# A reordering at both ends of the first gate and up stage: scale of h, slots of Wd's sums, half a row of plain products, W's fourth chunk

## The chip, the cores and the metric

The kernel runs on one core of a Trainium2 chip (trn2). The metric is the device time of one execution in microseconds, from runs on the chip; the profile is of one such execution. TensorE does the matrix products, VectorE, ScalarE and GpSimd the rest, and SyncE issues the transfers in the order of its program. Each engine executes its own instructions strictly in order and waits on semaphores.

## What is computed

For x of 8 × 256 tokens with 1024 features:

```
base   = x W^T                                   (1024 -> 1024)
logits = x Wr^T + 5 * one_hot(id)                (8 experts), top 2, softmax -> gates
y      = base + 2 * sum over experts of gate * (x A^T) B^T
h      = silu(y Wg^T) * (y Wu^T)                 (1024 -> 3584)
out    = x + h Wd^T                              (3584 -> 1024)
```

All of it has to come out at close to single precision. The large matrices Wg, Wu and Wd hold float16 values; y and h do not, so each is split into a high and a low float16 part.

## The kernel before

The 2048 tokens are worked in four blocks b = 0 to 3 of T = 512 columns. The order on TensorE is: routing and base of block 0, routing of block 1, then for each b the gate and up products (first_gateup for b = 0, gateup for the others), the base of block b + 1, and down(b).

**Gate and up.** There are 28 units n of two chunks of 128 rows (row 0 and row 1): an even unit has rows of Wg, an odd one of Wu. Each row takes eight matmuls 128x512 with the high part y_hi. The product with the low part y_lo is done in two ways. Units 0 to 15 do it plainly, eight more matmuls 128x512 a row. Units from PLAIN = 16 on do the two rows together by a scheme of seven block products (four matmuls 128x256 each), for which VectorE first makes sums of weight blocks (weight_sums, tile mixed) and of y_lo's blocks (y_sums, y_blocks): products_12, products_34 and products_576. Between them ScalarE takes two results out of PSUM (copy_12: into m1 and m32), VectorE combines (cross_34: into m32 and m45; cross_45: into m45), and GpSimd adds m1 and m32. product_high(n, 0) and product_high(n, 1) do the high products; the one for row 1 waits for cross_45 (s_45). complete(n, 0) and (n, 1) add the cross sums, and product() makes h in single precision (hf).

Unit 15 is plain but stands at the change of scheme: its low products come first, then plain_high(15, 0), products_12(16), plain_high(15, 1), products_34(16). products_12(16) waits for VectorE's first half of y_blocks (s_sum), products_34(16) for ScalarE's two copies (s_copy).

**Sums of Wd.** During units 3 to 14 VectorE also makes 20 sums of blocks of Wd (down_weight_sum, numbered 0 to 19) into the WD_SUMS = 4 slots of wd_sum, sum i into slot i % 4, and SyncE stores each to DRAM. Slots 2 and 3 stand at 174 and 177.5 KB, where m1, m32 and m45 lie (174 to 181 KB); slots 0 and 1 stand at 114 and 200 KB. So ScalarE waits, ahead of copy_12(16), until the last stores of slots 2 and 3 (sums 18 and 19) have landed. Sums 15 and 16 are made in step s = 12, sums 17 and 18 in step 13, sum 19 in step 14. Ahead of the load of x_raw SyncE waits for all of them (down_sums_stored).

**Scale of h.** h of block 0 gets a power of two from the largest weight. ScalarE sums squares of each unit's weights, VectorE takes the largest (own_weight, step 25), GpSimd reduces over partitions (L2203, s_wall), and VectorE makes scales from it (largest_weight, six short operations that first wait for s_wall). rescale(m) applies the scale to hf[m], high (late_high on ScalarE) makes h's high part and low (late_split on VectorE) the low one: 0 to 3 in the last step, 4 to 27 spread over base(1), by LATE. h_sums and last_h_sums then make the sums that down(0) needs.

**base(1).** W is loaded in chunks of 128 rows into four slots. Chunks 0 to 2 come early (EARLY_W = 3), chunk 3 is loaded once unit 27's products are all done (load_w(1, 3) waits for s_g and s_u), and chunk o >= 4 once the chunk that held its slot (o - 4) has been used. ScalarE scales a chunk (w_high, L1845 and L1846), GpSimd makes its low part (w_low, L2160), and TensorE does 24 matmuls with it (L875 to L877). Behind chunk 2 comes turn(1) (transposes, L774), then ScalarE's turned_high (L1876) and VectorE's turned_low (hgT_lo, L1303), which the matmuls of lora (L905 to L907) need.

Names in the profile: L958, L959 and L968 are plain products (L968 low ones of unit 15), L981 plain_high, L988 a block of the scheme, L1035 product_high, L1058 and L1065 the products of down.

Of the kernel before, what the change touches and what calls it, by code (L numbers as in the profile page):

```python
# [5 lines left out]
P = 128  # L6
# [9 lines left out]
F16 = mybir.dt.float16  # L16
# [23 lines left out]
WD_SUMS = 4  # L40
# [9 lines left out]
def adaln_ffn(nc, xT, ids, W, WrT, AT, BT, Wg, Wu, Wd, outT):  # L50
    NB, _, KC, _ = xT.shape
    OC = W.shape[0]
    MC = Wg.shape[0]
# [34 lines left out]
    MH = MC // 2  # L88
# [61 lines left out]
    with ExitStack() as ctx:  # L150
# [3 lines left out]
        def sb(name, kb, shape, dt):  # L154

            return nc.alloc_sbuf_tensor_at(name, shape, dt, offset=base_at + int(kb * KB))
# [27 lines left out]
        x_raw = sb("x_raw", 102, [P, KC, T], F32)  # L184
        x_lo = sb("x_lo", 102, [P, KC, T], F32R)
        wd_half = sb("wd_half", 86, [P, 2, 2, MC, P], F16)
        wd_sum = [sb(f"wd_sum{i}", kb, [P, MH, P], F16) for i, kb in enumerate((114, 200, 174, 177.5))]
        pieces = [sb(f"piece{i}", 135 + 3.5 * i if i < 2 else 86 + 3.5 * (i - 2), [P, MH, P], F16)
                  for i in range(PIECE_SLOTS)]
        xr = sb("xr", 103.5, [P, XR, T], F32)  # L190
# [517 lines left out]
        def _(pe):  # L708
# [231 lines left out]
            def first_gateup():  # L940
                for n in range(PLAIN - 1):
                    pe.wait_ge(d_gu[GU_SLOT[n]], 32 * GU_LOADS[n])
                    if n == 0:
                        for k in range(KC):
                            pe.wait_ge(s_ylo, k + 1)
                            for row in range(2):
                                bank, w, done = chunk(n, row, True)
                                MM(bank, w[:, k, :], y_hi[:, k, :], start=(k == 0), stop=False, skip_group_check=True)
                                mm = MM(bank, w[:, k, :], y_lo[:, k, :], start=False, stop=(k == KC - 1),
                                        skip_group_check=True)  # L950
                                if k == KC - 1:
                                    mm.then_inc(done, 1)
                        continue
                    unit_free(n)
                    for row in range(2):
                        bank, w, done = chunk(n, row, True)
                        for k in range(KC):
                            MM(bank, w[:, k, :], y_hi[:, k, :], start=(k == 0), stop=False)  # L958
                            mm = MM(bank, w[:, k, :], y_lo[:, k, :], start=False, stop=(k == KC - 1))  # L959
                        mm.then_inc(done, 1)  # L960

                n = PLAIN - 1
                pe.wait_ge(d_gu[GU_SLOT[n]], 32 * GU_LOADS[n])
                unit_free(n)
                for row in range(2):
                    bank, w, done = chunk(n, row, True)
                    for k in range(KC):
                        mm = MM(bank, w[:, k, :], y_lo[:, k, :], start=(k == 0), stop=False, skip_group_check=True)  # L968
                mm.then_inc(s_plain, 1)
                plain_high(n, 0)  # L970
                products_12(PLAIN)
                plain_high(n, 1)
                products_34(PLAIN)
                products_12(PLAIN + 1)
                products_576(PLAIN)
                by_blocks(PLAIN, MC)

            def plain_high(n, row):
                bank, w, done = chunk(n, row, True)
                for k in range(KC):  # L980
                    mm = MM(bank, w[:, k, :], y_hi[:, k, :], start=False, stop=(k == KC - 1), skip_group_check=True)  # L981
                mm.then_inc(done, 1)

            def block(bank, second, w, y, first):

# [158 lines left out]
        def _(dve):  # L1144
# [251 lines left out]
            def rescale(m):  # L1396
                V.tensor_scalar(hf[:, m], hf[:, m], wmax[:, 2:3], None, ALU.mult).then_inc(s_rs, 1)
# [204 lines left out]
            def first_gateup():  # L1602
                for s in range(MC):
                    blocks_next = PLAIN <= s + 1 < MC
                    if s == MC - 1:
                        rescale(0)
                        late_split(0, FIRST_LATE)
                    if s == PLAIN - 1:
                        dve.wait_ge(s_plain, 1)
                        y_blocks()  # L1610
                    if s >= PLAIN - 1:
                        for u in SUM_AT.get(s, ()):
                            weight_sums(u)
                    if blocks_next:
                        cross_34(s + 1)
                    if s == MC - 3:
                        own_weight()
                    if s >= PLAIN:
                        complete(s, 0)
                        complete(s, 1)  # L1620
                    elif s % 2:
                        for m in (s - 1, s):
                            dve.wait_ge(s_u, m + 1)
                            product(0, m, hf[:, m])
                    if s == MC - 2:

                        largest_weight()
                    if blocks_next:
                        cross_45(s + 1)
                    if s < PLAIN - 1:  # L1630
                        for u in SUM_AT.get(s, ()):
                            weight_sums(u)
                    if s == Y_SUMS_AT:
                        y_sums(0)
                    for q, c in DOWN_SUMS.get(s, ()):
                        down_weight_sum(q, c)
                    if s == SCALES_AT:
                        fine_scales()
# [171 lines left out]
        def _(act):  # L1810
# [79 lines left out]
            def late_high(first, end):  # L1890
                for m in range(first, end):
                    act.wait_ge(s_rs, m + 1)
                    if m >= WORK:
                        act.wait_ge(s_hlo, m - WORK + 1)
                    high(m, hf[:, m])

            def base(b):
                if b == 1:
                    late_high(FIRST_LATE, 6)
                else:  # L1900
                    route(b)
                w_high(b, 3)
                if b == 1:
                    late_high(6, 8)
                w_high(b, 4)
                if b == 1:
                    late_high(8, 9)
                turned_high(b)
                if b == 1:
                    late_high(9, 11)  # L1910
                w_high(b, 5)
                if b == 1:
                    late_high(11, LATE[0])
                for o in range(OC):
                    copy_chunk(b, o)
                    if o in (3, 4):
                        w_high(b, o + 3)
                    if b == 1:
                        late_high(LATE[o], LATE[o + 1])
                    if b == 0 and 2 <= o < 6:  # L1920
                        x1_high(2 * o - 4)
                        x1_high(2 * o - 3)
# [93 lines left out]
            def first_gateup():  # L2016
                for s in range(MC):
                    if 0 < s < PLAIN:
                        for u in SUM_AT.get(s, ()):
                            sum_squares(u)  # L2020
                    if s >= PLAIN:
                        if s % 2 == 0:
                            act.wait_ge(s_fix, 2 * nth(s) - 1)
                            silu(0, s)
                        if s + 2 < MC:
                            copy_12(s + 2)
                        if s % 2 == 0:
                            act.wait_ge(s_fix, 2 * nth(s))
                            silu(0, s + 1)
                        for u in SUM_AT.get(s, ()):  # L2030
                            sum_squares(u)
                    elif s % 2 == 0:
                        for m in (s, s + 1):
                            act.wait_ge(s_g, m + 1)
                            silu(0, m)
                    if s == 0:
                        sum_squares(0)
                    if s == PLAIN - 1:

                        for i in range(2, WD_SUMS):  # L2040
                            act.wait_ge(d_dsum[i], 16 * 5 * PAIRS // WD_SUMS)
                        copy_12(PLAIN)
                        copy_12(PLAIN + 1)
                    q, j = divmod(s - 1, 3)
                    if 0 <= q < PAIRS:
                        for i in ((0,), (1, 2), (3,))[j]:
                            halve_down(q, i)
                    next_parts(s)

                act.wait_ge(s_m6, nth(MC - 2))  # L2050
                act.wait_ge(d_mixed[2], 16 * mixed_stores(2))
                late_high(0, FIRST_LATE)
# [199 lines left out]
```

## Time and profile before

| | |
|---|---|
| time, median of 3 runs | 1331.1 us (1330.82, 1331.10, 1332.72) |
| time of the profiled execution | 1330.87 us |
| its span, first to last instruction | 1329.0 us |
| TensorE matmul busy | 1320.0 us (99% of the span), 8540 instructions |
| VectorE / ScalarE / GpSimd busy | 794.6 / 408.6 / 132.4 us |
| mean granted clock of TensorE | 0.998 |
| the chain that ended last | TensorE 98%, VectorE 1%, issue 1% |

The profiled execution took 1.87 us more than its span; that lies around the first and the last instruction. Times inside the profile are microseconds from the start of the span. The granted clock is the share of full speed (2.4 GHz) that the throttle let TensorE have: 1.00 is 2.4 GHz, 0.50 is 1.2 GHz.

### The profile page before, as it was taken

The page shows a single profiled execution, that of the slowest core. Times are in us where ns is not written, and L with a number is a line of the kernel's source. Part 1 is how long each engine was busy: PE and PEld are TensorE (multiplying, and loading weights), DVE is VectorE, ACT ScalarE, POOL GpSimd, SP SyncE. Part 2 cuts the span into 40 slices and gives each one's busy share as a digit, 9 for nine tenths or more (in the row PEclk, how much of TensorE's full clock was granted, in tenths as well). Part 3 has the DMA queues.
Part 4 walks back from the last instruction along what each step waited for, and adds up shares of the span by engine and source line. Part 5 has one row for each costly group of instructions (what it writes and reads, how often), then busy time and mean ns, then how long its engine had stood idle before and what let it go on. Part 6 is the DMA issues. An engine that isn't in the chain of part 4 may idle for free.

```text
span 1329.0 us, 22089 instructions
## 1 busy us (share of the span) xinstructions
PE 1320.0 (99%) x8540; PEld 860.5 (65%) x8540; DVE 794.6 (60%) x1540; ACT 408.6 (31%) x705; POOL 132.4 (10%) x163
## 2 busy tenths in 40 slices
PE   9999999999999999999999999999999999999999
PEld 7854456545666666677667666667666666666666
DVE  7798888678614577764742555556473255545612
ACT  4368845563101344321011223332110122222000
POOL 3200202241000011100000111110000011111000
PEclk9999999999999999999999999999999999999999
DMA  8379985225955778853794568653387465666564
GB/s 309 119 258 358 410 310 180 76 80 198 320 203 157 275 256 322 314 183 111 262 322 157 186 223 275 185 165 114 103 310 268 144 186 184 186 181 205 172 233 137
DMA packets 117528, 287.00 MB, mean 216 GB/s; under 512 B 14128, under 2 KB 16816, under 8 KB 116656
## 3 DMA queue, kind: packets, MB, share of 16 engines
q1 hardware_dynamic: 117136, 285.43, 62.7%
q8 instruction: 68, 1.11, 0.4%
q14 instruction: 36, 0.29, 0.1%
q10 hardware_dynamic: 288, 0.16, 0.0%
HBM read 241.24 MB, written 44.30 MB: 215 GB/s over the span
## 4 chain that ended last, share of the span: by engine, by line
PE 98%; DVE 1%; issue 1%; DMA 0%; POOL 0%; ACT 0%; DVEq 0%; ACTq 0%; POOLq 0%
PE banks L1035 25%; PE banks L988 22%; PE banks L1058 14%; PE banks L1065 13%; PE banks L782 4%; PE banks L959 3%; PE banks L958 3%; PE banks L834 2%; PE banks L878 1%; PE banks L880 1%; PE banks L879 1%; PE banks L875 1%; PE banks L877 1%; PE banks L876 1%; PE banks L1094 1%; PE banks L718 1%
## 5 line engine op out<-in xcount | busy, mean ns | idle before, releaser
L1035 PE MATMUL banks<-y_hi,gu_ring 128*128 128x512 f16 x1504 | 355.7, 381 | 2.8 <-DVE m L1662 2.8
L1035 PEld LDWEIGHTS banks<-y_hi,gu_ring 128*128 128x128 f16 x1504 | 147.3, 98 | 143.2 <-DVE m L1662 3.3
L1058 PE MATMUL banks<-h,piece 128*128 128x512 f16 x840 | 188.5, 380 | 0.0
L1935 ACT ACTIVATE sg<-banks,sc 128x512 f32<-128x512 f32 x112 | 76.4, 686 | 211.6 <-DVE banks L1671 153.6
L2181 POOL TENSOR_TENSOR m<-m,m 128x256 f32<-128x256 f32 x96 | 69.7, 726 | 717.4 <-DVE m L1652 717.3
L1058 PEld LDWEIGHTS banks<-h,piece 128*128 128x128 f16 x840 | 82.1, 98 | 89.8
L1674 DVE TENSOR_TENSOR banks<-banks,m 128x256 f32<-128x256 f32 x96 | 41.5, 432 | 137.2 <-PE banks L1035 137.0
L1065 PE MATMUL banks<-h,piece 128*128 128x256 f16 x896 | 106.2, 273 | 0.0
L1065 PEld LDWEIGHTS banks<-h,piece 128*128 128x128 f16 x896 | 87.6, 98 | 19.8
L988 PE MATMUL banks<-y_lo,gu_ring 128*128 128x256 f16 x752 | 97.5, 273 | 1.5 <-ACT m L2065 1.5
L2064 ACT COPY m<-banks 128x256 f32<-128x256 f32 x96 | 35.3, 368 | 173.0 <-PE banks L988 166.8
L988 PE MATMUL banks<-y_sum,mix_c 128*128 128x256 f16 x672 | 87.1, 273 | 0.0
L1652 DVE TENSOR_TENSOR m<-banks,m 128x256 f32<-128x256 f32 x96 | 40.3, 420 | 68.0 <-PE banks L988 68.0
L988 PEld LDWEIGHTS banks<-y_lo,gu_ring 128*128 128x128 f16 x752 | 73.4, 98 | 11.2 <-issue 2.0
L959 PE MATMUL banks<-y_lo,gu_ring 128*128 128x512 f16 x208 | 79.0, 380 | 0.0
L958 PE MATMUL banks<-y_hi,gu_ring 128*128 128x512 f16 x208 | 79.0, 380 | 0.0
L1065 PE MATMUL banks<-h_sum,piece 128*128 128x256 f16 x672 | 78.6, 273 | 0.0
L1888 ACT ACTIVATE h<-work 128x512 f16<-128x512 f32 x84 | 52.9, 630 | 82.0 <-DVE work L1599 82.0
L1065 PEld LDWEIGHTS banks<-h_sum,piece 128*128 128x128 f16 x672 | 65.7, 98 | 7.7
L988 PEld LDWEIGHTS banks<-y_sum,mix_c 128*128 128x128 f16 x672 | 65.7, 98 | 7.7
L2097 ACT ACTIVATE d<-banks 128x256 f32<-128x256 f32 x16 | 6.1, 379 | 204.1 <-PE banks L1065 191.0
L1599 DVE SCALAR_TENSOR_TENSOR work<-banks,sc,sg 128x512 f32<-128x512 f32 x84 | 63.1, 751 | 3.0
(239 smaller groups left out, 1959.3 us busy)
## 6 DMA issues: line engine op xcount, KB each, us to landing
piece<-down_dram SPq DMA_DIRECT2D x80, 448.0 KB, 5.5
mix_c<-mix_dram SPq DMA_DIRECT2D x84, 384.0 KB, 4.0
piece<-Wd SPq DMA_DIRECT2D x64, 448.0 KB, 5.4
gu_ring<-Wu SPq DMA_DIRECT2D x110, 256.0 KB, 3.3
gu_ring<-Wg SPq DMA_DIRECT2D x108, 256.0 KB, 3.2
mix_a<-mix_dram SPq DMA_DIRECT2D x84, 256.0 KB, 2.7
mix_dram<-mixed SPq DMA_DIRECT2D x28, 640.0 KB, 5.1
wb<-w_dram SPq DMA_DIRECT2D x64, 256.0 KB, 3.7
```

The source lines that it names most:

```text
L782: mm = MM(bank[:, at], w[a][:, k, :], x[:, a, k, :], start=(first and a == 0 and k == 0), stop=False, skip_group_check=True)
L958: MM(bank, w[:, k, :], y_hi[:, k, :], start=(k == 0), stop=False)
L959: mm = MM(bank, w[:, k, :], y_lo[:, k, :], start=False, stop=(k == KC - 1))
L988: mm = MM(bank[:, at], w[:, k, :], y[:, k, :], start=(first and k == 0), stop=False, skip_group_check=True)
L1035: mm = MM(bank, w[:, k, :], y_hi[:, k, :], start=False, stop=(k == KC - 1), skip_group_check=True)
L1058: mm = MM(bank, w[:, k, :], h[:, half * MH + k, 0, :], start=(start and k == 0), stop=False, skip_group_check=True)
L1065: mm = MM(bank[:, at], w[:, k, :], y[:, k, :], start=(start and k == 0), stop=False, skip_group_check=True)
L1599: V.scalar_tensor_tensor(out=tile, in0=banks[:, chunk_bank(b, m, 1), :], scalar=sc[:, b, 2:3], in1=sg[:, n % SG, :], op0=ALU.mult, op1=ALU ...
L1674: V.tensor_tensor(odd_1, odd_1, m45[:, n % 2], ALU.add).then_inc(s_fix, 1)
L1888: S.mul(h[:, m, 0, :], source, 1.0 / LO_SHIFT).then_inc(s_hhi, 1)
L1935: S.activation(sg[:, n % SG, :], banks[:, chunk_bank(b, m, 0), :], ACT.Silu, scale=sc[:, b, 1:2]).then_inc(s_sg, 1)
L2181: G.tensor_tensor(m1[:, n % 3], m1[:, n % 3], m32[:, n % 2], ALU.add).then_inc(s_1236, 1)
```

## The change

Four things are moved; no instruction is added or removed.

1. The four slots of wd_sum trade places: slots 0 and 1 now stand where m1 and m32 lie, slots 2 and 3 at 114 and 200 KB; ScalarE waits ahead of copy_12(16) for the stores of slots 0 and 1.
2. TensorE does the first four of the eight matmuls of plain_high(15, 1) ahead of products_12(16), and the other four behind it.
3. VectorE calls largest_weight at the start of the last step (s = 27), behind cross_45(27), where it stood ahead of cross_45(27).
4. In base(1) ScalarE scales W's chunk 3 ahead of late_high(4) to late_high(7), where it stood between 5 and 6.

```diff
-        wd_sum = [sb(f"wd_sum{i}", kb, [P, MH, P], F16) for i, kb in enumerate((114, 200, 174, 177.5))]
+        wd_sum = [sb(f"wd_sum{i}", kb, [P, MH, P], F16) for i, kb in enumerate((174, 177.5, 114, 200))]
...
-                plain_high(n, 0)
+                plain_high(n, 0, 0, KC)
+                plain_high(n, 1, 0, KC // 2)
                 products_12(PLAIN)
-                plain_high(n, 1)
+                plain_high(n, 1, KC // 2, KC)
                 products_34(PLAIN)
...
-            def plain_high(n, row):
+            def plain_high(n, row, first, end):
                 bank, w, done = chunk(n, row, True)
-                for k in range(KC):
+                for k in range(first, end):
                     mm = MM(bank, w[:, k, :], y_hi[:, k, :], start=False, stop=(k == KC - 1), skip_group_check=True)
-                mm.then_inc(done, 1)
+                if end == KC:
+                    mm.then_inc(done, 1)
...
                     if s == MC - 1:
+
+                        largest_weight()
                         rescale(0)
                         late_split(0, FIRST_LATE)
...
-                    if s == MC - 2:
-
-                        largest_weight()
                     if blocks_next:
                         cross_45(s + 1)
...
             def base(b):
-                if b == 1:
-                    late_high(FIRST_LATE, 6)
-                else:
+                if b == 0:
                     route(b)
                 w_high(b, 3)
                 if b == 1:
-                    late_high(6, 8)
+                    late_high(FIRST_LATE, 8)
                 w_high(b, 4)
...
                     if s == PLAIN - 1:
 
-                        for i in range(2, WD_SUMS):
+                        for i in range(2):
                             act.wait_ge(d_dsum[i], 16 * 5 * PAIRS // WD_SUMS)
                         copy_12(PLAIN)
```

## Rows read from the trace of the kernel before

**Rows 1.** Waits of TensorE, whole execution: total us, times, longest.

```profile
PE banks L1035 <- DVE m L1662: 2.8, 1, 2.8
PE banks L988 <- ACT m L2065: 1.5, 1, 1.5
```

**Rows 2.** Windows: length, busy PE, PEld, DVE, ACT, POOL, then clock, DMA, GB/s.

```profile
184.00:190.00 6.00, 5.00 (x41) 3.89 (x42) 3.98 (x10) 1.32 (x4) 0.72 (x1) 1.00 0.81 292
260.69:263.65 2.96, 0.16 (x1) 0.00 (x1) 1.51 (x8) 0.00 (x0) 0.41 (x1) 0.91 0.00 0
263.65:266.78 3.13, 3.13 (x8) 1.13 (x9) 2.75 (x7) 1.78 (x3) 0.00 (x0) 0.54 0.00 0
266.78:271.94 5.16, 5.16 (x25) 2.35 (x24) 5.05 (x11) 1.94 (x4) 0.00 (x0) 1.00 0.33 102
```

**Rows 3.** Timeline, 178 to 186 us: start, us, engine, line, operation, [idle before, releaser].

```profile
178.48 1.89 PE L981 MATMUL banks<-y_hi,gu_ring 128*128 128x512 f16 x8
...
180.60 0.61 PE L988 MATMUL banks<-y_sum,mixed 128*128 128x256 f16 x4 [0.23 <-DVE y_lo L1373]
...
181.49 1.89 PE L981 MATMUL banks<-y_hi,gu_ring 128*128 128x512 f16 x8
...
183.59 0.42 DVE L1582 TENSOR_TENSOR mixed<-halved 128x512 f16<-128x512 f16 x1
184.09 0.37 ACT L2064 COPY m<-banks 128x256 f32<-128x256 f32 x1 [6.29 <-DMA down_dram<-wd_sum]
...
184.36 0.39 ACT L2065 ACTIVATE m<-banks 128x256 f32<-128x256 f32 x1
...
184.89 1.03 PE L988 MATMUL banks<-y_lo,gu_ring 128*128 128x256 f16 x8 [1.51 <-ACT m L2065]
...
185.96 0.42 DVE L1652 TENSOR_TENSOR m<-banks,m 128x256 f32<-128x256 f32 x1 [1.95 <-PE banks L988]
```

**Rows 4.** Timeline, 172 us: the stores of sums 17 and 18 as issued.

```profile
172.50 1.32 SPq L474 DMA_DIRECT2D down_dram<-wd_sum  x2
```

**Rows 5.** DMA issues from 172.45 and in 255 to 315 us: KB each, us to landing.

```profile
down_dram<-wd_sum SPq DMA_DIRECT2D x2, 448.0 KB, 5.1
...
w_raw<-W SPq DMA_DIRECT2D x5, 512.0 KB, 3.2
```

**Rows 6.** Timeline, 258 to 267 us, around unit 27's last row.

```profile
258.09 1.04 PE L988 MATMUL banks<-y_sum,mixed 128*128 128x256 f16 x8
...
258.96 1.89 PE L1035 MATMUL banks<-y_hi,gu_ring 128*128 128x512 f16 x8
261.49 0.41 POOL L2203 PARTITION_ALL_REDUCE wmax<-wmax  x1 [5.86 <-issue]
...
263.17 0.42 DVE L1662 TENSOR_TENSOR m<-m,banks 128x256 f32<-128x256 f32 x1
...
263.65 3.29 PE L1035 MATMUL banks<-y_hi,gu_ring 128*128 128x512 f16 x8 [2.80 <-DVE m L1662]
```

**Rows 7.** Timeline, 270 to 284 us: VectorE, ScalarE and GpSimd in base(1).

```profile
270.75 0.49 DVE L1397 TENSOR_SCALAR hf<-hf,wmax 128x512 f32<-128x512 f32 x1
...
271.80 1.14 ACT L1845 ACTIVATE w<-w_raw,mx 128x1024 f16<-128x1024 f32 x1
...
274.06 6.78 POOL L2160 TENSOR_TENSOR w<-w_raw,w 128x256 f16<-128x256 f32 x8 [12.17 <-ACT w_raw L1846]
...
275.20 0.89 DVE L1397 TENSOR_SCALAR hf<-hf,wmax 128x512 f32<-128x512 f32 x1
...
283.68 0.75 DVE L1303 SCALAR_TENSOR_TENSOR hgT_lo<-banks,y_sc,hgT_hi 128x512 fp32r<-128x512 f32 x1 [4.62 <-ACT hgT_hi L1876]
```

**Rows 8.** VectorE's timeline, and one piece of the chain of waits.

```profile
313.82 2.03 DVE L1714 TENSOR_TENSOR h_sum<-h 128x3584 f16<-128x3584 f16 x1 [0.69 <-PE banks L877]
...
327.50 1.09 DVE L1727 TENSOR_SCALAR h<-h 128x3584 f16<-128x3584 f16 x1
...
331.11 6.11 PE banks L1065 x56
```

## The prediction

> **What bounds the kernel now.** I read the page first. TensorE is busy 1320.0 us of a span of 1329.0 us (the table above), so the kernel is one long stream of matmuls and only 9.0 us of it are idle. An edit that adds and removes no matmul can win only from those 9.0 us, and from stretches in which the matmuls run slower than elsewhere. The view of waits, kept to TensorE, says where the idle time is [rows 1]: one wait of 2.8 us before the matmuls of L1035 (for VectorE's m45) and one of 1.5 us before those of L988 (for ScalarE's copies). The rest is a start-up, the tail behind the last matmul and a few tenths. Both waits stand in stage b = 0, the edited one. The table of windows then shows what the first wait costs beyond itself [rows 2]: between 260.69 and 263.65 us TensorE does next to nothing, and in the 3.13 us behind it the granted clock is 0.54, so mostly the 1.2 GHz level, under eight matmuls; from 266.78 us it is 1.00 (2.4 GHz) again, 24 matmuls in 5.16 us, 0.216 us each. Behind the 1.5 us wait the clock is 1.00 at once [rows 2]. So the second stall is worth more than its 2.8 us.
>
> **Part one: first blocks (slots of Wd's sums, half a row of plain products).** TensorE begins unit 15's plain high products at 178.48 us, does eight, waits briefly for y_lo and does products_12(16) at 180.60, does the other eight from 181.49, and starts products_34(16) only at 184.89 [rows 3]. That last start waits for ScalarE's pair of copies at 184.09 and 184.36, and ScalarE waited 6.29 us for a store of wd_sum [rows 3]: slots 2 and 3 lie where m1 and m32 are written, and their last user is sum 19, stored last.
> After the edit m1 and m32 lie on slots 0 and 1, last used by sums 16 and 17. The store of 17 is one of the two issued from 172.50 us, which take 5.1 us to land [rows 4, 5]: with 1.32 us for the issuing of both, by 178.9 at the latest. ScalarE then waits for products_12(16) alone. Its new place: 12 matmuls of 0.216 behind 178.48, so 181.07. VectorE's first doubled y_lo released TensorE at 180.60 before, so that wait of 0.23 us goes. Eight matmuls of 0.109 (180.60 to 181.49, with 0.02 of change-over) end at 181.94. From the end of a block to the engine that reads it take 0.20 us (184.89 plus 0.87 is 185.76; VectorE starts at 185.96 [rows 3]): ScalarE starts at 182.14. The two copies take 0.66 us (184.09 to 184.36 + 0.39), and 0.14 us later TensorE started: 182.94. Meanwhile the four plain matmuls that are left run from 181.94 to 182.80 and hide all but 0.14 us of the copies. Gain: 184.89 − 182.94 = **1.95 us**. Without any wait it were 184.89 − 182.80 = 2.09, the upper bound. The lower bound is 0: if sums 16 and 17 landed no sooner than sum 19 did, ScalarE's copies would start at 184.09 as before.
> What is late next? VectorE's cross_34(16) needs TensorE's block, now out at 182.94 + 0.87 + 0.20 = 184.01, and VectorE's sums of the weights end at 183.59 + 0.42 = 184.01 [rows 3]. They meet; a few hundredths at most. SyncE's queue is blocked till the last sum has landed in either version, so the load of unit 20's weights and x_raw stay at 184.1 to 184.5 in absolute time; what uses them is VectorE's work some 9 us and more later, so the shift of 1.95 us costs nothing there.
>
> **Part two: largest_weight behind cross_45(27).** VectorE executes in order. Before, it stood in front of largest_weight until GpSimd's all-reduce, which starts at 261.49, and only after six short operations did it write m45 (263.17), which released TensorE's last row at 263.65 [rows 6]. But m45's own inputs were there early: the seventh product's four matmuls end at 258.09 + 0.44, and 0.20 later, at 258.73, VectorE can do its 0.42 us: 259.15. TensorE reaches the row at 258.96 + 1.73 = 260.69, so 1.5 us later: no wait. The row then runs 260.69 to 262.42 at the full clock, where before the next product began at 266.78. Gain: 2.96 (263.65 − 260.69) for the stall and 3.13 − 1.73 = 1.40 for the clock [rows 2], together **4.36 us**. Bounds: 2.96, if the clock drops all the same; 4.36 above. The stall of 1.5 us that left the clock alone [rows 2] is longer than anything I expect to remain, so I take 4.36.
> By the Trainium skill (TensorE: Matmul & The Clock Gate, What's actually happening) the clock level follows how busy TensorE has recently been, and by its note there the moment of a switch varies from run to run. By that rule some runs of before may have missed the drop, and against those the gain here is 2.96. The rows show one run only, with the drop.
>
> **Does base(1) let the gain through?** The all-reduce at 261.49 follows GpSimd's own last operation by 5.86 us [rows 6], so it should move with the stream; if it stayed where it is in absolute time, VectorE would be 1.95 us later still, which the reserve worked out below would have to bear. As it is, largest_weight ends just before 263.17 as before (first gain left aside), and VectorE's work behind it comes only 0.35 us sooner (m45 has left its place), while TensorE is 4.36 sooner. VectorE is thus 4.0 us later than before relative to TensorE. Who needs it? The products by W of chunks 0 to 2 need neither h nor the split. The turn of hg and VectorE's hgT_lo come next: there VectorE had been idle 4.62 us [rows 7], which pays for the 4.0.
> The fourth chunk of W: its load is issued when TensorE's last row is done, 262.6, and lands 3.2 us later [rows 5], 265.9. Before, late_high of 4 and 5 stood ahead of its scaling on ScalarE, and the scaling began at 271.80, two passes of 1.1 us. Now it comes directly behind late_high(3). VectorE hands over a rescale per 1.0 us from 263.2 on (a rescale and a low part each), so that is about 267.1; the scaling ends at 269.3, and GpSimd's subtraction (3.4, half of the eight in 6.78 [rows 7]) at 272.7. TensorE wants it at 262.42 + 3 × 5.16 = 277.9 at the earliest. Without the move the scaling would follow rescale(5), which VectorE does at 270.4, and GpSimd would be done at about 276.9, still in time: the move is worth nothing by itself.
> But the move puts that GpSimd work beside VectorE's products and splits. A rescale took 0.49 us alone and 0.89 beside GpSimd [rows 7]. Three or four operations with 0.4 each are 1.3 us. Step by step: VectorE's rescale(5) at 270.4, then a pair of operations per 1.0 us, low(8) behind late_high(8) at 276.2, end 276.9 without and about 278.4 with this contention. hgT_lo is due at 283.68 − 4.36 = 279.3. Reserve 0.9 to 2.4 us. Behind it stand 0.69 us of VectorE's wait at h_sum and the time from its last sum, 327.50 + 1.09 = 328.6, to TensorE's L1065 at 331.1, 2.5 us [rows 8]: 3.2 us more before TensorE would feel it. So cost 0.
> By the Trainium skill (SBUF — State Buffer, SBUF: two separate sides) VectorE and GpSimd share a port pair under an exclusive lock, and the loser is blocked for a whole instruction. By it VectorE might lose all 3.4 us, reach hgT_lo 1.0 us late, and use a third of the 3.2 behind it; the sum stays, the reserve shrinks. The trace agrees so far as the rescale's 0.89 for 0.49 goes.
> Behind 316 us all loads and waits hang on TensorE's own progress, so both gains go through to the end.
>
> **Sum.** 1.95 + 4.36 = 6.3 us. The profiled execution took 1330.87 us, of which 1329.0 span: 1324.6 and a span of 1322.7. The median of the runs lies 0.2 higher, so **1324.8 us**.
>
> **Rivals.**
> (a) The first stall stays, since the wait on slots 0 and 1 ends late or VectorE's sums hold cross_34 back. Against it: 3 us of reserve on the stores. 1331.1 − 4.4 = 1326.7. Chance 0.06.
> (b) The clock falls all the same, or part of the runs never had the drop: 1331.1 − 1.95 − 2.96 = 1326.2. For it, the times of before reach from 1330.82 to 1332.72, and only one of its executions shows a clock. Chance 0.05.
> (c) The time goes into base(1): VectorE's chain of splits, which has little idle time there, arrives late and TensorE waits at L1065 for what it had gained. It needs a delay of 0.9 + 3.2 us and more behind what I reckoned, and 4.4 more to take all: 1329.1. Chance 0.06.
> (d) Slower: ScalarE now stands at the chunk's load ahead of all late splits. If it landed late, late_high(4) and so VectorE's chain would stand still with it. From 267.1 on each microsecond goes into the reserve of about 4 (0.9 + 3.2) and then into TensorE's wait. To eat 6.3 and be 2.7 slower it must land 13 us behind 267.1, 17 us after issue instead of 3.2, while the queues are nearly empty there (DMA share 0.33 [rows 2]). At that point 1333.8. Chance 0.02.
> The forecast holds the other 0.81.
>
> **Range.** The forecast's own range is 1324.0 (the last waits gone too, and 0.5 of scatter) to 1325.6. With (a) and (b) it reaches 1327.2; (c) and (d) are left out. A difference under 0.2%, 2.7 us, can't be told from no change here. Faster: forecast, (a), (b), 0.92. Same: (c), 0.06. Slower: (d), 0.02.
>
> **What the profile of the changed kernel would show.** The wait of 2.8 us at L1035 gone from TensorE's waits, that of 1.5 us down to about 0.1 to 0.3; ScalarE's first copy near 182.1, released by TensorE and not by a store; products_34(16) at 182.9; the last row of unit 27 near 258.7 (260.69 − 1.95) with clock 1.00; the first product by W near 260.5; VectorE's idle time before hgT_lo down from 4.62 to between 0.5 and 2.5; TensorE busy 1.4 us less. Wrong would be: a new TensorE wait at L877, L905, L1058 or L1065 between 270 and 330 us, a clock below 1.00 behind 255 us, or a copy still released by wd_sum.

## The result, and the profile after

The changed kernel takes 1325.07 us (median of 6 runs, 1324.31 to 1325.22), the kernel before beside it 1331.0 (6 runs, 1329.53 to 1332.72). The ratio is 0.9954, with a 95% interval of 0.9941 to 0.9967: 5.9 us faster. The forecast was 1324.8.

On the page, TensorE's busy time has gone from 1320.0 to 1317.6 us, with the same 8540 matmuls:

```profile
span 1323.4 us, 22089 instructions
...
PE 1317.6 (100%) x8540; PEld 860.7 (65%) x8540; DVE 793.6 (60%) x1540; ACT 408.9 (31%) x705; POOL 132.1 (10%) x163
```

TensorE's waits over the whole execution, which answer to [rows 1]:

```profile
PE banks L714 <- DVE idle L1772: 1.2, 1, 1.2
PE banks L718 <- DVE x_lo L1179: 0.9, 1, 0.9
```

Both waits of before are gone from the list (ahead of products_34(16) some 0.2 us of idle time are left, 183.30 behind the end of four matmuls from 182.22). What is left is the start-up. In the profiled execution of before the twelve warm-up matmuls (L714) took 5.30 us and covered the second row's wait for x; in this one they took 4.34. That accounts for 1.0 of the 2.4 us of busy time that are gone; the other 1.4 is the slow clock behind the last row. The start-up comes before anything that the change touches. Unit 15's plain high products begin at 178.75 here, where they began at 178.48 [rows 3]: the profiled execution is 0.27 us late before the change begins, so the stages are compared from a start of their own.

**The first blocks.** The timeline, which answers to [rows 3]:

```profile
178.75 2.75 PE L982 MATMUL banks<-y_hi,gu_ring 128*128 128x512 f16 x12
...
181.34 0.60 PE L990 MATMUL banks<-y_sum,mixed 128*128 128x256 f16 x4
...
182.22 1.03 PE L982 MATMUL banks<-y_hi,gu_ring 128*128 128x512 f16 x4
182.49 0.37 ACT L2063 COPY m<-banks 128x256 f32<-128x256 f32 x1 [4.41 <-PE banks L990]
...
182.76 0.39 ACT L2064 ACTIVATE m<-banks 128x256 f32<-128x256 f32 x1
...
183.30 1.03 PE L990 MATMUL banks<-y_lo,gu_ring 128*128 128x256 f16 x8
...
184.37 0.42 DVE L1653 TENSOR_TENSOR m<-banks,m 128x256 f32<-128x256 f32 x1
```

ScalarE's first copy is now released by TensorE (L990), not by a transfer. From the first plain high product to products_34(16) it is 183.30 − 178.75 = 4.55 us, where it was 184.89 − 178.48 = 6.41: 1.86 us gained, 1.95 forecast.

**The last row of unit 27 and base(1).** The timeline, which answers to [rows 6] and [rows 7]:

```profile
256.49 1.04 PE L990 MATMUL banks<-y_sum,mixed 128*128 128x256 f16 x8
...
257.13 0.42 DVE L1663 TENSOR_TENSOR m<-m,banks 128x256 f32<-128x256 f32 x1 [0.44 <-PE banks L990]
257.37 3.62 PE L1037 MATMUL banks<-y_hi,gu_ring 128*128 128x512 f16 x16
259.98 0.41 POOL L2202 PARTITION_ALL_REDUCE wmax<-wmax  x1 [5.95 <-issue]
...
265.60 1.13 ACT L1846 ACTIVATE w<-w_raw,mx 128x1024 f16<-128x1024 f32 x1
...
267.86 3.19 POOL L2159 TENSOR_TENSOR w<-w_raw,w 128x256 f16<-128x256 f32 x4 [7.47 <-ACT w_raw L1847]
...
269.37 1.15 DVE L1404 SCALAR_TENSOR_TENSOR h<-h,hf 128x512 f16<-128x512 f16 x1
...
270.44 0.89 DVE L1399 TENSOR_SCALAR hf<-hf,wmax 128x512 f32<-128x512 f32 x1
...
277.72 0.75 DVE L1305 SCALAR_TENSOR_TENSOR hgT_lo<-banks,y_sc,hgT_hi 128x512 fp32r<-128x512 f32 x1 [1.35 <-ACT hgT_hi L1877]
```

VectorE begins to write m45 at 257.13, before TensorE has begun even the first of the two rows, and is done at 257.55, 1.55 us before the second row begins (1.5 forecast); the sixteen matmuls of both rows stand in one line (x16) with no wait between them. The windows of the two rows and of what follows (columns as in [rows 2]) show the clock at 1.00 throughout:

```profile
257.37:259.10 1.73, 1.73 (x11) 0.79 (x9) 0.18 (x1) 0.04 (x1) 0.00 (x0) 1.00 0.00 0
259.10:260.82 1.72, 1.72 (x9) 0.78 (x8) 0.33 (x3) 0.00 (x0) 0.41 (x1) 1.00 0.00 0
260.82:264.00 3.18, 3.18 (x16) 1.47 (x15) 2.66 (x9) 1.15 (x2) 0.00 (x0) 1.00 0.50 164
```

From the first row's start to the first product by W it is 3.45 us, where it was 266.78 − 258.96 = 7.82: 4.37 us gained, 4.36 forecast. The all-reduce moved with the stream, as assumed: 259.98 − 257.37 = 2.61 us behind the first row, where it was 2.53. And VectorE's idle time before hgT_lo is 1.35 us where it was 4.62, inside the 0.9 to 2.4 forecast; the rows at 269.37 and 270.44 are the operations that GpSimd's earlier work stretches.

**What arrives.** The starts of the four down stages in the chain of waits, first of the kernel before:

```profile
314.42 3.04 PE banks L1094 x14
...
637.83 3.04 PE banks L1094 x14
...
961.23 3.04 PE banks L1094 x14
...
1234.67 3.02 PE banks L1094 x14
```

and of the changed kernel:

```profile
308.49 3.04 PE banks L1096 x14
...
631.89 3.04 PE banks L1096 x14
...
955.30 3.04 PE banks L1096 x14
...
1229.01 3.02 PE banks L1096 x14
```

The lead is 5.93, 5.94 and 5.93 us: it passes base(1) and two whole stages without a loss, and it is the sum of 1.86 and 4.37, less the 0.27 of the late start and 0.03 that I did not place. Between 955 and 1229 another 0.27 us is lost: the stationary loads before a piece's matmuls (L1067) wait 0.4 us there for nothing that the trace names.

### The profile page after: what moved, and what is told of

The parts are those of the page before. It is cut to its first block, busy times and chain, and to the rows that moved or that the text cites. A ratio compares the mean times of both kernels' runs of the same rounds, so it can differ in the third digit from the quotient of the medians.

```text
span 1323.4 us, 22089 instructions
## 1 busy us (share of the span) xinstructions
PE 1317.6 (100%) x8540; PEld 860.7 (65%) x8540; DVE 793.6 (60%) x1540; ACT 408.9 (31%) x705; POOL 132.1 (10%) x163
## 4 chain that ended last, share of the span: by engine, by line
PE 99%; DMA 0%; DVE 0%; SPq 0%; issue 0%; ACT 0%; DVEq 0%
PE banks L1037 25%; PE banks L990 22%; PE banks L1060 14%; PE banks L1067 13%; PE banks L782 4%; PE banks L958 4%; PE banks L959 4%; PE banks L834 2%; PE banks L878 1%; PE banks L880 1%; PE banks L879 1%; PE banks L875 1%; PE banks L876 1%; PE banks L877 1%; PE banks L1096 1%; PE banks L718 1%
## 5 line engine op out<-in xcount | busy, mean ns | idle before, releaser
L1067 PE MATMUL banks<-h,piece 128*128 128x256 f16 x896 | 106.1, 273 | 0.0
L1067 PEld LDWEIGHTS banks<-h,piece 128*128 128x128 f16 x896 | 87.7, 98 | 19.8
L990 PE MATMUL banks<-y_lo,gu_ring 128*128 128x256 f16 x752 | 97.4, 273 | 0.1
L990 PE MATMUL banks<-y_sum,mix_c 128*128 128x256 f16 x672 | 87.1, 273 | 0.0
L990 PEld LDWEIGHTS banks<-y_lo,gu_ring 128*128 128x128 f16 x752 | 73.5, 98 | 9.7 <-issue 0.5
L1067 PE MATMUL banks<-h_sum,piece 128*128 128x256 f16 x672 | 78.6, 273 | 0.1
L1067 PEld LDWEIGHTS banks<-h_sum,piece 128*128 128x128 f16 x672 | 65.7, 98 | 8.0 <-issue 0.4
L990 PEld LDWEIGHTS banks<-y_sum,mix_c 128*128 128x128 f16 x672 | 65.8, 98 | 7.6
```

The source lines that it names most:

```text
L990: mm = MM(bank[:, at], w[:, k, :], y[:, k, :], start=(first and k == 0), stop=False, skip_group_check=True)
L1067: mm = MM(bank[:, at], w[:, k, :], y[:, k, :], start=(start and k == 0), stop=False, skip_group_check=True)
```

## The experiments

The small numbers need the runs' clocks. Each run lists the mean granted clock of its execution, to three digits. Over four sets, the kernel before was executed 69 times beside the experiments: 23 executions have a clock of 1.000 and a median of 1329.56 us (1328.92 to 1330.15); 46 have 0.997 to 0.999 and 1331.30 (1330.59 to 1333.05). There is no overlap. So the kernel before has two times, 1.7 us apart, and its median lies among the commoner ones. The mean clock does not say where in an execution the clock fell. The profiles of before, e5 and e6 show it at the wait ahead of unit 27's last row, and where that wait is gone or filled in whole or half (the changed kernel, e2, e3, e4, e7, e8, e9, e11, e12) no execution is below 1.000, save three of e10, which has long waits of its own. So the fall is put down to that wait in the other executions too; no trace of those shows it.

| kernel | time, us (range, runs) | runs at clock 1.000 | ratio, 95% interval |
|---|---|---|---|
| e1 first blocks only | 1329.24 (1327.85 to 1330.47, 11) | 3 of 11 | 0.9991, 0.9982 to 1.0 |
| e2 largest_weight only | 1326.57 (1326.43 to 1326.97, 6) | 6 of 6 | 0.9968, 0.9956 to 0.998 |
| e3 wait filled, 13 matmuls | 1329.62 (1329.39 to 1330.21, 11) | 11 of 11 | 0.9991, 0.9982 to 1.0 |
| e4 changed kernel again | 1324.65 (1324.44 to 1325.45, 5) | 5 of 5 | 0.9955, 0.9942 to 0.9969 |
| e5 slots only | 1329.88 (1327.48 to 1331.34, 10) | 1 of 10 | 0.9994, 0.9985 to 1.0004 |
| e6 half row only | 1330.97 (1329.34 to 1331.57, 10) | 1 of 10 | 1.0003, 0.9993 to 1.0012 |
| e7 whole row ahead | 1325.35 (1325.13 to 1325.6, 5) | 5 of 5 | 0.9963, 0.9949 to 0.9977 |
| e8 fourth chunk not moved | 1324.75 (1324.33 to 1325.11, 4) | 4 of 4 | 0.9956, 0.9939 to 0.9973 |
| e9 VectorE 3.7 us later | 1324.88 (1324.71 to 1325.13, 4) | 4 of 4 | 0.9958, 0.9942 to 0.9975 |
| e10 VectorE 7.4 us later | 1328.84 (1328.4 to 1329.95, 10) | 7 of 10 | 0.9987, 0.9978 to 0.9997 |
| e11 wait half filled | 1329.51 (1329.02 to 1330.31, 10) | 10 of 10 | 0.9987, 0.9977 to 0.9996 |
| e12 VectorE 5.6 us later | 1326.37 (1326.27 to 1327.07, 5) | 5 of 5 | 0.9962, 0.9948 to 0.9976 |

**The two parts apart, and together (e1, e2, e4).** e1 is the kernel before with items 1 and 2 of the change, e2 the kernel before with item 3:

```diff
                     if s == MC - 1:
+
+                        largest_weight()
                         rescale(0)
...
-                    if s == MC - 2:
-
-                        largest_weight()
```

> The first-blocks part alone (slots of Wd's sums and half a row of plain products), largest_weight and W's fourth chunk left as in the kernel before. My theory: products_34(16) starts 1.9 us sooner behind the first plain high product than before, the 2.8 us wait at the last row and the slow clock behind it stay, time 1331.0 - 1.9 = 1329.1. Rival (the two stalls are one: with the first gone the second grows, since the all-reduce stays where it is in absolute time): last row's wait 4.8 us, time 1331.

> largest_weight behind cross_45(27) alone, all else as before. My theory: wait of 2.8 us gone, clock 1.00 there, first product by W 4.4 us sooner relative to product_high(27, 0), time 1331.0 - 4.4 = 1326.6. Rival (the clock falls there all the same, whatever TensorE waited): 3.0 us sooner, 1328.0. Rival (base(1) gives it back): 1331.

> The changed kernel as it is, beside its parts on the same chip. If the parts add: the gains of the two single parts, 1.9 and 4.4, sum to its 6.3 less the scatter, 1324.8 to 1325.1. Rival (they overlap): less than the sum by over 1 us.

Measured: 1329.24, 1326.57 and 1324.65 beside 1331.1 of before: gains of 1.9, 4.5 and 6.4 us. By these medians the parts add.

The medians mix executions that kept the clock with others, so they have to be compared like with like. In this set the kernel before has 1329.54 at clock 1.000 (8 executions) and 1331.36 below it (14). e2 gains 2.97 us on the first, which is the stall alone, and 4.8 on the second. e1 gains 1.5 us at clock 1.000 (3 executions, 1328.05) and 1.6 below it (8, 1329.72), not 1.9; the changed kernel gains 4.9 and 6.7. So e1's median of 1329.24 is in part the luck of how many of its executions kept the clock.

e1's profiled execution was one that kept it, and shows what the profile of before could not:

```profile
PE banks L1037 <- DVE m L1664: 3.0, 1, 3.0
```

That is its wait; this is the row of matmuls behind it:

```profile
262.23 1.90 PE L1037 MATMUL banks<-y_hi,gu_ring 128*128 128x512 f16 x8 [3.04 <-DVE m L1664]
```

The wait is even 0.24 us longer than in [rows 6], but the eight matmuls take 1.90 us, not 3.29. That fits e1's smaller gain: 1.87 us from its first blocks (178.58 to 183.12 in its trace, 4.54 us) less 0.24 is 1.6. Its all-reduce came 2.76 us behind the first row's start at 257.31, where it came 2.53 behind before:

```profile
260.07 0.41 POOL L2205 PARTITION_ALL_REDUCE wmax<-wmax  x1 [6.09 <-issue]
```

The stall did not grow by the 1.9 us that e1's rival expected. So behind a wait of about 3 us the clock falls in some executions and in others it does not, and the longer of these two waits is the one that left it alone. In e5's profiled execution it fell early and stayed low longer; its windows from the wait on:

```profile
260.90:263.50 2.60, 1.32 (x4) 0.50 (x5) 2.08 (x8) 0.87 (x2) 0.00 (x0) 0.58 0.00 0
263.50:266.00 2.50, 2.50 (x8) 0.85 (x7) 2.50 (x6) 1.50 (x3) 0.00 (x0) 0.50 0.00 0
266.00:268.00 2.00, 2.00 (x6) 0.75 (x5) 1.96 (x4) 0.67 (x2) 0.00 (x0) 0.50 0.51 190
268.00:270.00 2.00, 2.00 (x10) 0.89 (x9) 1.93 (x5) 0.21 (x1) 0.00 (x0) 0.97 0.18 72
```

There the clock is at the 1.2 GHz level until 268, so the first six products by W are slow too. The last row of that profile begins at 262.18 and the first product at full speed at 268.12: fourteen matmuls in 5.9 us, where the full clock needs 3.0, so 2.9 us are lost. In e6's profile two products by W are slow beside the row, and 1.7 us are lost. The price of this one wait thus reaches from 0 to about 3 us beyond the wait, in the four profiles that have it: 0 (e1), 1.4 (before), 1.7 (e6) and 2.9 (e5).

**The wait filled with work (e3, e11).** To part the clock from the wait, useless matmuls into a free bank, ahead of the wait for m45:

```diff
             def product_high(n, row):
                 bank, w, done = chunk(n, row, True)
+                if row and n == MC - 1:
+                    pe.wait_ge(s_wlo, OC)
+                    pe.wait_ge(s_xlo, 2 * KC)
+                    pe.wait_ge(s_hf, MC - 2)
+                    for i in range(13):
+                        MM(banks[:, 7, :], w16[:, 0, 0, i % KC, :], x16[:, 1, i % KC, :], start=True, stop=True)
                 if row:
                     pe.wait_ge(s_45, nth(n))
```

e11 has `range(6)`.

> The kernel before with 13 matmuls 128x512 of no use (into a free PSUM bank) put into the wait ahead of the last row of unit 27; the wait for m45 stays. If the idle time is what lowers the clock: granted clock 1.00 behind it, the eight matmuls of the last row in 1.7 us in place of 3.1, time 1.4 less than before (1329.6), with TensorE busy about 1.4 us more. Rival (the clock falls for another reason there, or the 2.8 us wait alone is the cost): the last row stays at 3.1 us and the time at 1331.0.

> The kernel before with 6 useless matmuls in place of 13 ahead of the last row of unit 27: 1.3 us of the wait are filled, some 1.5 us of idle time stay, as long as the other wait of before (1.5 us at L988), which left the clock alone. My theory: the clock stays at 1.000 in all executions and the time is that of the filled kernel, 1329.6, narrow. Rival (any wait at this place lowers the clock in part of the executions): some executions at 0.998 to 0.999 and 1331, as before.

The timeline of e3 around the wait:

```profile
260.91 2.97 PE L1037 MATMUL banks<-x,w 128*128 128x512 f16 x13
...
263.77 1.90 PE L1041 MATMUL banks<-y_hi,gu_ring 128*128 128x512 f16 x8
```

m45 still comes when it came (the last row starts 4.59 us behind the first one's start at 259.18, where it was 4.69 before), and yet 13 matmuls more make the kernel 1.5 us faster: 1329.62. That is the time of the executions of before that kept their clock, 1329.56. All 11 executions kept it, where 23 of 69 do without the filling. With half the filling (e11) there is a wait again:

```profile
PE banks L988 <- ACT m L2071: 1.5, 1, 1.5
PE banks L1041 <- DVE m L1668: 1.4, 1, 1.4
```

with the row behind it at full speed:

```profile
263.83 1.90 PE L1041 MATMUL banks<-y_hi,gu_ring 128*128 128x512 f16 x8 [1.42 <-DVE m L1668]
```

and all 10 executions keep the clock (1329.51). So at this place the unfilled wait, 2.78 to 3.04 us long where a profile shows it, lowers the clock in 46 of 69 executions, and 1.4 us of idle time in none of ten.

**What in the first blocks does it (e5, e6, e7).** e5 is the kernel before with the slots traded and ScalarE's wait on them, e6 the kernel before with the half row alone, and e7 the changed kernel with

```diff
                 plain_high(n, 0, 0, KC)
-                plain_high(n, 1, 0, KC // 2)
+                plain_high(n, 1, 0, KC)
                 products_12(PLAIN)
-                plain_high(n, 1, KC // 2, KC)
```

> The kernel before with the slots traded (and ScalarE's wait on slots 0 and 1), but no half row. My theory: ScalarE's copies start when products_12(16) is done, near 182.0 us with products_12 at 180.6; products_34(16) starts when the plain row ends, about 4.7 us behind the first plain high product where it was 6.4: gain 1.65 to 1.7 us, so the slots carry nearly all of part one. Rival (the half row is what hides the copies): gain under 1.0.

> The kernel before with half a row of plain products ahead of products_12(16), slots as before. My theory: products_34(16) still starts 0.8 us behind ScalarE's first copy, which the store of sum 19 releases near 184.1: gain 0 (the 0.24 us wait for y_lo goes and comes back in the wait for the copies). Rival: gain 0.2 to 0.4.

> The changed kernel with the whole second plain row ahead of products_12(16), nothing left behind it. My theory: nothing covers the copies, so products_34(16) waits for them: products_12(16) ends at +4.33 us behind the first plain high product, copies end 0.28 + 0.66 + 0.14 later: +5.4 where the changed kernel has 4.55, that is 0.85 us slower than it. Rival (cross_34, not the copies, is the bound): no slower.

Their times scatter with the clock (e5's median is 0.8 us under that of before, e6's 0.3 over it, and both intervals hold 1), so the trace decides. From the first plain high product to products_34(16), e5:

```profile
178.55 1.89 PE L981 MATMUL banks<-y_hi,gu_ring 128*128 128x512 f16 x8
...
183.27 1.04 PE L988 MATMUL banks<-y_lo,gu_ring 128*128 128x256 f16 x8
```

e6:

```profile
178.90 2.75 PE L982 MATMUL banks<-y_hi,gu_ring 128*128 128x512 f16 x12
...
184.47 0.37 ACT L2066 COPY m<-banks 128x256 f32<-128x256 f32 x1 [6.24 <-DMA down_dram<-wd_sum]
...
185.27 1.03 PE L990 MATMUL banks<-y_lo,gu_ring 128*128 128x256 f16 x8 [1.88 <-ACT m L2067]
```

e7:

```profile
178.09 3.62 PE L981 MATMUL banks<-y_hi,gu_ring 128*128 128x512 f16 x16
...
183.50 1.03 PE L989 MATMUL banks<-y_lo,gu_ring 128*128 128x256 f16 x8 [0.92 <-ACT m L2063]
```

These are 4.72, 6.37 and 5.41 us, beside 6.41 before and 4.55 after. The slots alone give 1.69 of the 1.86 us; the half row alone turns the short wait for y_lo into a longer one for the copies and gives 0.04; behind the slots it gives the other 0.17. The whole row leaves nothing to hide the copies and loses 0.86 us, as expected (0.85); its time is 0.6 us over e8's and 0.3 to 0.7 over the changed kernel's two medians.

**The fourth chunk (e8).** The changed kernel with item 4 undone: late_high(4) and (5), then the chunk, then (6) and (7).

> The changed kernel with W's fourth chunk scaled between late_high(5) and late_high(6), as before. My theory: GpSimd has it ready near 275.0 and TensorE wants it near 276.3 (stream 1.9 us sooner than before): no wait, time as the changed kernel, 1324.9. Rival (the move is needed): a wait of TensorE at L877 and its neighbours of some 1 to 3 us.

1324.75 us, no wait of TensorE. Its GpSimd row and VectorE's hgT_lo:

```profile
272.26 6.79 POOL L2161 TENSOR_TENSOR w<-w_raw,w 128x256 f16<-128x256 f32 x8 [11.84 <-ACT w_raw L1847]
```

```profile
277.92 0.75 DVE L1305 SCALAR_TENSOR_TENSOR hgT_lo<-banks,y_sc,hgT_hi 128x512 fp32r<-128x512 f32 x1 [0.66 <-ACT hgT_hi L1877]
```

Half of the eight is done at about 275.7; TensorE wants the chunk behind the turn, near 277. The move is worth no time here, but it takes the chunk from 1.3 us ahead of its use to 5.7, and leaves VectorE 1.35 us ahead of hgT_lo where it would have 0.66. GpSimd's work stands beside VectorE's splits without the move as well: in e8 VectorE's four operations from 273.41 on take 0.89, 1.15, 0.89 and 1.16 us.

**How much base(1) can bear (e9, e12, e10).** The changed kernel with four, six or eight of these ahead of base(1):

```diff
+                    if s == MC - 1:
+                        for _ in range(4):
+                            step(V.memset(bm45[:], 0.0))
```

> The changed kernel with four memsets of 128x768 (useless work, some 0.8 us each by the length of other VectorE operations, 3.4 us in all) on VectorE behind unit 27's products, ahead of base(1): it measures the reserve. The changed kernel's rows leave 1.35 us of VectorE's wait at hgT_lo, 0.68 at h_sum and 2.5 from the last sum to TensorE's L1067, 4.5 us. My theory: 3.4 is under 4.5, so no TensorE wait and the time stays at 1324.8 to 1325.1. Rival (the splits are already the bound, or some consumer is nearer): a TensorE wait between 270 and 330 us and 1 to 3.5 us more.

> The same with eight memsets, some 6.8 us. My theory: the 4.5 us of reserve are used up and TensorE waits for the rest, about 2.3 us, at L1067 (for last_h_sums): time 1327.2, more by up to 1.6 in executions in which the clock falls behind the wait. Rival (each part of the chain catches up in its own waits): no TensorE wait, 1325.

> The changed kernel with six memsets, 5.6 us (0.93 us each, as measured with four and eight). From four (3.7 us, no wait) and eight (7.4 us, 3.8 us lost): if VectorE's hgT_lo and ScalarE's copies behind it are the nearest consumers, about 2 us lost, waits at L905 and L875: 1327.0. Rival (the reserve I had reckoned, 4.5 us up to L1067, and the rest of the loss comes from something that eight memsets alone disturb): 1.1 us or less lost.

One memset costs 0.93 us with its wait, so the delays are 3.7, 5.6 and 7.4 us. Against 1324.9 (the mean of the changed kernel's two medians) they cost 0.0, 1.5 and 3.9 us. In e10 three of ten executions have a clock below 1.000 (1329.75 to 1329.95); the seven that kept it have a median of 1328.60, which is 3.7 us. The wait that appears first, in e12:

```profile
PE banks L875 <- ACT y_raw L1888: 1.7, 1, 1.7
```

and in e10:

```profile
PE banks L875 <- ACT y_raw L1888: 2.1, 1, 2.1
...
PE banks L905 <- DVE hgT_lo L1305: 1.1, 1, 1.1
```

So the reserve is about 4 us (5.6 − 1.5 and 7.4 − 3.9 make 4.1 and 3.5), and it ends at the fifth chunk's products (L875), which wait for ScalarE's copy of chunk 0 (L1888), held up in ScalarE's queue by the late splits; then at lora (L905). In e12 the copies begin at 286.22 and the product follows 0.71 us later:

```profile
286.93 0.38 PE L875 MATMUL banks<-x,w 128*128 128x512 f16 x1 [1.72 <-ACT y_raw L1888]
```

In e9 they begin at 283.83 and the product stands at 284.56, 0.73 us later and without a wait: by the traces the 3.7 us of e9 use up all but a few hundredths of the reserve. Neither L875 nor L905 is the place that I had reckoned the reserve from.

## Why the prediction was right, point by point

- **First blocks, 1.95 us.** Right; 1.86 in the trace, 1.9 in e1's median (1.5 to 1.6 like with like, since e1's stall was 0.24 us longer). The missing 0.1 is ScalarE's start behind products_12(16): 0.28 us behind its end (181.34 + 0.87 to 182.49), where I had taken VectorE's 0.20 for it. Rival (a) is out.
- **What is late next: cross_34(16).** It met, as said: the next wait did not grow.
- **Stall and clock, 2.96 + 1.40 = 4.36 us.** In the profiled executions 4.37; that close a hit owes something to luck, since the forecast took the clock's price, 1.40, from the one execution that it is compared with. As a term for the median it was right too (4.5 in e2), but its second half was taken for a constant and is none: e1's profile and the 69 executions show 0 in one execution of three and about 1.7 in the others, up to about 3. That is the second half of rival (b), which I gave 0.05: it was true of a third of the runs, not enough to move the median of before much. Its price of 1326.2 was wrong as well: executions of before that keep the clock make the gain smaller, not the changed kernel slower. Its first half, that the clock falls all the same, did not occur.
- **base(1) lets it through.** Right: no TensorE wait, the lead is the same at 308 as at 955 us. The reserve ahead of hgT_lo was 1.35 us, between the 0.9 and 2.4 forecast. But those bounds took the moved GpSimd work as a cost to VectorE of up to 1.5 us, and e8 has the opposite sign: without the move the reserve is 0.7 us smaller. And "3.2 us more" at h_sum and L1065 was the wrong place: e12 and e10 find the first wait at L875 and L905, by way of ScalarE's queue. The size, 0.9 + 3.2 = 4.1 forecast and 3.5 to 4.1 measured by times and 3.7 by the traces, came out near by luck. Rivals (c) and (d) are out for this kernel.
- **The lock on a shared port** (the Trainium skill, SBUF — State Buffer, SBUF: two separate sides). The trace fits in direction: beside GpSimd the rescale takes 0.89 and the low part 1.15 us, where 0.48 and 0.69 are their times alone, and GpSimd's four subtractions take 3.19 us beside them and 2.56 in e9, beside VectorE's memsets. In size it is far from the 3.4 us that the forecast drew from the rule as the worst case: the two operations shown lose 0.9 us together. Each loses less than one subtraction's 0.64 us (2.56 / 4), so these rows do not contradict a block for the rest of one instruction either. And e8, where GpSimd's work stands where it stood before, has 0.66 us left of hgT_lo's 4.62: that is the shift of 4.0 as reckoned, and the move of the chunk gives 0.7 back to it.
- **The move of the fourth chunk is worth nothing by itself.** Right (e8).
- **The sum.** 6.3 forecast, 5.9 beside the first set and 6.4 beside e4's. The profiled execution lost 0.27 us at its start and 0.27 late, at places that the change doesn't touch. The 6.3 holds for the mix of executions that before had: against its executions at clock 1.000 (1329.56) the two sets of the changed kernel gain 4.5 and 4.9 us, which is 1.95 + 2.96 = 4.9 without the clock's term, and against the others (1331.30) 6.2 and 6.7.

## What to carry to other kernels

Where one engine is busy 99% of the time, read its few waits and then the clock behind each: a wait long enough to lower TensorE's clock can cost more than its length, and filling it with useless matmuls is worth trying even if the wait can't be removed (1.5 us at the median in e3). Where a kernel has two times, compare executions of like clock, or the mix passes for an effect. Move a wait for a late value behind whatever the busiest engine needs from the same queue, and lay buffers so that the last writer of a slot isn't the last of the whole series. To know how much lateness a side engine can bear, delay it and see which wait comes up first; reckoning along one engine's own rows misses the consumers that hang behind another queue.

## What the runs showed of the hardware that I had not expected

- The same wait lowers TensorE's granted clock in 46 of 69 executions and leaves it at 1.000 in 23, with two separate sets of times, 1331.30 and 1329.56 us. Its length is known from profiles alone: 2.78 us (e6), 2.80 (before) and 2.95 (e5) with a fall, 3.04 (e1) without. By the Trainium skill (TensorE: Matmul & The Clock Gate, What's actually happening) the moment at which the clock switches varies between runs of one kernel, which it shows for the rise at a kernel's start; here it is the fall behind a wait that varies.
- Only 1 of 10 executions of e5 and of e6 kept the clock, where 23 of 69 of the kernel before did, and 8 of the 20 in the same set. So few executions may differ by chance; why, if they do differ, stays open.
- 1.4 us of idle time at the same place lowered it in none of 10 (e11), and e12's 1.7 us at L875 in none of 5. e10, with 2.1 us there and 1.1 at L905, has it below 1.000 in 3 of 10.
- The all-reduce on GpSimd starts 5.75 to 6.09 us behind GpSimd's last operation in all fourteen profiles, though its input has long been there (VectorE wrote it at 249.0 in the profile of before); that time moves with the stream, and the trace names nothing that it waits for.
